# Layer three of a graph network: edge tables in two fp16 terms with a lift per feature, ten gathered tiles a block instead of eleven

## The reference

```python
h_edge = concatenate([h[src], h[dst]], axis=-1)
m_ij = relu(h_edge @ W_interact + b_interact)            # one row per edge
m_i = segment_sum(m_ij, src, num_segments=6250) / sqrt(16)
x = x + (h + relu((h + m_i) @ W_update + b_update))      # h + ... is the layer's own residual
```

## Time and profile before

| | |
|---|---|
| time, median of 3 runs | 1647.03 us (1644.14 to 1647.19) |
| the profiled execution: time, span | 1644.32 us, 1642.5 us |
| TensorE, matmuls | 1429.2 us busy, 87% |
| VectorE | 1394.0 us, 85% |
| ScalarE | 1009.9 us, 61% |
| GpSimd | 999.7 us, 61% |
| granted TensorE clock, mean | 0.952 of full speed |

### The profile page before, as it was taken

One profiled execution on the slowest core, in us unless ns is written; L12 is line 12 of the kernel. 1 busy time (PEld: TensorE's weight loads), 2 busy tenths in 40 slices (PEclk: granted clock), 3 DMA queues, 4 the chain that ended last, 5 costly groups with the idle time before them and its releaser, 6 DMA issues. The chain is left out here.

```text
span 1642.5 us, 43233 instructions
## 1 busy us (share of the span) xinstructions
PE 1429.2 (87%) x16208; PEld 1228.5 (75%) x16208; DVE 1394.0 (85%) x4293; ACT 1009.9 (61%) x1990; POOL 999.7 (61%) x1033
## 2 busy tenths in 40 slices
PE   1614888999999989999996499999999999999997
PEld 1302666777777667777776499999999999999997
DVE  7968797999999347777767599999999999999997
ACT  1724676787778520000005388888888878788885
POOL 4363606787850027777702677777777777777773
PEclk9855899999999999999997799999999999999999
DMA  3004725564653169999961244444454444444442
GB/s 114 1 1 120 277 105 195 196 240 173 223 209 134 29 203 300 301 309 306 292 204 35 71 114 115 122 113 123 114 123 121 115 116 112 113 121 115 122 115 61
DMA packets 125002, 245.15 MB, mean 149 GB/s; under 512 B 21784, under 2 KB 76201, under 8 KB 124794
## 3 DMA queue, kind: packets, MB, share of 16 engines
q1 hardware_dynamic: 95179, 184.46, 33.6%
q0 software_dynamic: 28032, 57.34, 14.0%
q10 hardware_dynamic: 1584, 0.59, 0.1%
HBM read 172.37 MB, written 73.14 MB: 149 GB/s over the span
## 5 line engine op out<-in xcount | busy, mean ns | idle before, releaser
L1427 PE MATMUL ps<-slab,room 125*128 125x128 bf16 x6762 | 435.6, 219 | 0.0
L987 ACT ACTIVATE slab<-ps 128x980 f16<-128x980 f32 x256 | 321.3, 1277 | 118.3 <-PE ps L1200 103.1
L1427 PEld LDWEIGHTS ps<-slab,room 125*128 125x128 bf16 x6762 | 393.1, 98 | 0.0
L899 POOL DMA_INDIRECT cells<-b_rows,work x319 | 305.8, 959 | 97.0 <-issue 91.4
L1099 ACT ACTIVATE lnw<-iota_w,keys 128x126 f32<-128x126 f32 x900 | 290.9, 389 | 1.6 <-POOL slab L890 1.6
L1418 PE MATMUL ps<-inv,hot 125*128 125x128 bf16 x2700 | 260.5, 221 | 3.7 <-DVE hot L2097 3.7
L1211 PE MATMUL ps<-slab,room 128*128 128x320 f16 x1568 | 252.2, 301 | 0.1
L1227 PE MATMUL ps<-slab,room 128*128 128x320 f16 x1568 | 225.0, 299 | 0.0
L1200 PE MATMUL ps<-hot 128*128 128x245 bf16 x1024 | 161.7, 283 | 49.3 <-DVE hot L1765 38.5
L859 POOL DMA_INDIRECT hot<-t_rows,pairs x160 | 165.7, 1036 | 51.7 <-issue 48.2
L1227 PEld LDWEIGHTS ps<-slab,room 128*128 128x128 f16 x1568 | 152.6, 98 | 58.3 <-issue 2.7
(11 more groups left out here) (346 smaller groups left out, 2284.4 us busy)
## 6 DMA issues: line engine op xcount, KB each, us to landing
slabs_d<-slab SPq DMA_DIRECT2D x14, 3920.0 KB, 13.2
slab<-slabs_d SPq DMA_DIRECT2D x98, 560.0 KB, 5.2
hot<-lane_d SPq DMA_DIRECT2D x50, 576.0 KB
keys<-up_d SPq DMA_DIRECT2D x50, 128.0 KB
inv<-inv_row SPq DMA_DIRECT2D x32, 160.0 KB
cells<-b_rows,work POOLq DMA_INDIRECT x319
keys<-down_d SPq DMA_DIRECT2D x50, 96.0 KB
t_rows<-room SPq DMA_DIRECT2D x1, 3200.0 KB, 13.7
```

Source lines behind the costliest of these rows:

```text
L899: p.indirect_dma_start(rows_g[gi % RS][:, j, :], None, b_rows, bass.IndirectOffsetOnAxis(ap=node_t[:, t:t + 1], axis=0)).then_inc(e_gath[g ...
L987: a.activation(slab[par][:, :, u * UB * BW:(u + 1) * UB * BW].rearrange("p h (k d) -> p k h d", k=UB), psum_unit(u).rearrange("p k (h d) - ...
L1427: last = t.matmul(to, end_hot[g // 3][0:BN, u:u + P], bt[0:BN, bt_at(tile, w), k, :], start=False, stop=w == w1 - 1 and k == TERMS - 1)
```

## The change

The tables of layer three come in two fp16 terms instead of three bf16 ones (`a_terms`, `bt`: the high term and what is left). So that fp16's range suffices, each feature is multiplied by a power of two: `lift_of_edges` on VectorE makes the powers from the norms of the columns of `W_interact` and the bias and multiplies the weights and the bias by them, and `keep_sum` divides by them again, and by the 4 of sqrt(16). The one-hots of lanes and ends are fp16.

Tile 4 is picked too: 8 tiles are picked, 10 fetched. The messages of groups 0, 2 and 5 (`SPLIT_GROUPS`) are two fp16 terms with an fp16 one-hot; those of groups 1, 3 and 4 are plain f32 with an f32 one-hot, without a low term. VectorE instead of ScalarE makes the one-hots of the source of groups 2 and 5 (`DVE_HOTS`). The lanes' one-hots are made in one piece of 2304 columns. The high term of a block's `a` is made by ScalarE, the low one by VectorE. In the preparation, ScalarE's middle term and one of GpSimd's two subtractions go.

```diff
-    GROUPS = (((0,), (4, 5)), ((1,), (6, 7)), ((2, 3), (8,)), ((15,), (9, 10)), ((16,), (11, 12)), ((17,), (13, 14)))
-    UP, DOWN = (0, 1, 2, 3), (15, 16, 17)
+    GROUPS = (((0, 1), (5,)), ((2, 3), (6,)), ((4,), (7, 8)), ((15,), (9, 10)), ((16,), (11, 12)), ((17,), (13, 14)))
+    UP, DOWN = (0, 1, 2, 3, 4), (15, 16, 17)
+    SPLIT_GROUPS = (0, 2, 5)
+    DVE_HOTS = (2, 5)
...
@@ ScalarE, second_layer
+                    if (s, u) == (1, 2):
+                        a.activation(edge_sq, w_ab[:, :], ACT.Square).then_inc(u_lift, 1)
+                    if (s, u) == (1, 9):
+                        act.wait_ge(s_once, ONCE_REACH)
+                        a.activation(edge_sq, ps[:, 2, 0:2 * D], ACT.Sqrt, scale=EDGE_REACH).then_inc(u_lift, 1)
@@ TensorE, second_layer
+                        if (s, u) == (1, 5):
+                            pe.wait_ge(u_lift, 4)
+                            t.matmul(ps[:, 2, 0:2 * D], ones[:, :], edge_sq, start=True, stop=True).then_inc(s_once, 1)
+                        if (s, u) == (2, 0):
+                            pe.wait_ge(u_lift, 5)
@@ VectorE, second_layer
+                        if (s, u) == (1, 13):
+                            lift_of_edges()
@@ VectorE
+            def lift_of_edges():
+                dve.wait_ge(u_lift, 5)
+                link(v.scalar_tensor_tensor(out=drop_f, in0=b_i, scalar=-1.0, in1=b_i, op0=ALU.mult, op1=ALU.max))
+                link(v.tensor_tensor(out=lift_f, in0=edge_sq[:, 0:D], in1=edge_sq[:, D:2 * D], op=ALU.add))
+                link(v.tensor_tensor(out=lift_f, in0=lift_f, in1=drop_f, op=ALU.add))
+                link(v.tensor_scalar(lift_f, lift_f, 1e-30, 1e30, ALU.max, ALU.min))
+                link(v.tensor_scalar(drop_b, lift_b, 23, None, ALU.arith_shift_right))
+                link(v.tensor_scalar(lift_b, drop_b, -1.0, float(2 * 127 + TOP), ALU.mult, ALU.add))
+                link(v.tensor_scalar(drop_b, drop_b, -float(TOP + 2), None, ALU.add))
+                link(v.tensor_scalar(lift_b, lift_b, 23, None, ALU.logical_shift_left))
+                link(v.tensor_scalar(drop_b, drop_b, 23, None, ALU.logical_shift_left))
+                for k in range(2):
+                    v.tensor_tensor(out=w_ab[:, k * D:(k + 1) * D], in0=w_ab[:, k * D:(k + 1) * D], in1=lift_f, op=ALU.mult)
+                v.tensor_tensor(out=b_i, in0=b_i, in1=lift_f, op=ALU.mult)
+                link(v.tensor_tensor(out=edge_sq[:, 0:D], in0=drop_f, in1=ident[:, :], op=ALU.mult))
+                link(v.tensor_reduce(out=settle[:, :], in_=edge_sq[:, 0:D], op=ALU.add, axis=AX.X))
+                nc.vector.sem_inc(u_lift, 1)
...
-                    for k in range(GB):
-                        piece = row_lane[0:BN, b % 2, k * GW:(k + 1) * GW]
-                        last = v.tensor_scalar(piece, piece, up_c[0:BN, 0:1], None, ALU.is_equal)
-                    last.then_inc(e_rowhot, 1)
+                    lanes_of = row_lane[0:BN, b % 2, :]
+                    v.tensor_scalar(lanes_of, lanes_of, up_c[0:BN, 0:1], None, ALU.is_equal).then_inc(e_rowhot, 1)
...
+            def source_hot(gi):
+                if gi % GB not in DVE_HOTS:
+                    return
+                if gi > 5:
+                    dve.wait_ge(e_psum, gi - 5)
+                b, at = gi // GB, DVE_HOTS.index(gi % GB)
+                both = [P, GT, BE // 2, 2]
+                v.tensor_tensor(out=src_hot[gi % 6].rearrange("p j (w e) -> p j w e", e=2),
+                                in0=iota_hi[:, 0:BE].rearrange("p (w e) -> p w e", e=2).unsqueeze(1).to_broadcast(both),
+                                in1=lane_twice[:, b, at, :, :].unsqueeze(2).to_broadcast(both), op=ALU.is_equal
+                                ).then_inc(e_dvehot, 1)
...
             for gi in range(NGR):
                 b, g = divmod(gi, GB)
                 add_rows(gi)
                 if gi + AHEAD < NGR:
                     prepare(gi + AHEAD)
                 low_term(gi)
-                if g < 2 and b + 1 < NB:
-                    split_a(b + 1, 2 * g)
-                    split_a(b + 1, 2 * g + 1)
+                if gi + AHEAD < NGR:
+                    source_hot(gi + AHEAD)
+                if g == 2 and b + 1 < NB:
+                    split_lo(b + 1)
@@ TensorE, edge_sum and source_sum
-                    for k in range(TERMS):
+                    for k in range(HALVES):
                         last = t.matmul(to, lanes_of, a_terms[0:BN, b % 2, k, :],
...
                 for j in range(GT):
-                    last = t.matmul(ps[0:BE, 4 + b % 2, 0:2 * D], src_hot[gi % 6][:, j, :],
-                                    msg[gi % 3][:, j, :, :].rearrange("p k f -> p (k f)"),
+                    of = msg_split[gi % 3][:, j, :, :].rearrange("p k f -> p (k f)") if split else msg[gi % 3][:, j, :]
+                    last = t.matmul(ps[0:BE, 4 + b % 2, 0:2 * D if split else D], src_hot[gi % 6][:, j, :], of,
@@ GpSimd, preparation
-                    p.tensor_tensor(out=brest[0:BN, bk % 2, :, :], in0=bslot[0:BN, c % 2, :, :], in1=to[:, :, 0, :],
-                                    op=ALU.subtract).then_inc(f_brest, 1)
-                if bk is not None:
-                    pool.wait_ge(f_bmid, bk + 1)
-                    p.tensor_tensor(out=to[:, :, 2, :], in0=brest[0:BN, bk % 2, :, :], in1=to[:, :, 1, :],
+                    p.tensor_tensor(out=to[:, :, 1, :], in0=bslot[0:BN, c % 2, :, :], in1=to[:, :, 0, :],
                                     op=ALU.subtract).then_inc(f_blo, 1)
```

More of the change, by code:

```diff
@@ L63, in gnn_kernel @@
     REACH = 260.0
-    assert LIFT * LIFT * D < 65504.0 ** 2 and REACH > 2 * D
+    EDGE_REACH = 130.0
+    assert LIFT * LIFT * D < 65504.0 ** 2 and REACH > 2 * D and EDGE_REACH > D
     MAGIC = 12582912.0
@@ L356, in gnn_kernel @@
-        a_rest = scaled[:, D:2 * D]
-        assert TERMS * D <= 2 * SC and 2 * D <= SC
+        bt_all = slab[1][:, :, :].rearrange("p h n -> p (h n)")
+        bt = bt_all[:, 0:BTN * HALVES * D].rearrange("p (t k f) -> p t k f", k=HALVES, f=D)
+        o, o1 = 2 * NB * D, BTN * HALVES * D + 2 * GW
+        end_hot = [room_b.bitcast(f16)[:, o:o + HOT_UNITS[0] * P], bt_all[:, o1:o1 + HOT_UNITS[1] * P]]
+        assert o + HOT_UNITS[0] * P <= NT * TERMS * P and o1 + HOT_UNITS[1] * P <= HI * SC
+        assert NT * D + GW <= HI * SC // 2 and KU * FH + 8 + GW <= 3 * KW // 2
@@ new lines, in gnn_kernel @@
+        msg_f = [slab_f[0][:, NT * D:NT * D + GW], work[:, KU * FH + 8:KU * FH + 8 + GW],
+                 slab_f[1][:, BTN * HALVES * D // 2:BTN * HALVES * D // 2 + GW]]
+        msg = [x.rearrange("p (j f) -> p j f", j=GT) for x in msg_f]
+        msg_split = [x.bitcast(f16).rearrange("p (j k f) -> p j k f", j=GT, k=2) for x in msg_f]
+        row_lane = hot_b.bitcast(f16)[:, 0:2 * CAP].rearrange("p (s n) -> p s n", s=2)
+        a_kept = table_f[:, 0:NB * D].rearrange("p (t f) -> p t f", f=D)
@@ L521, in chunk, with splits, hots @@
             return hT[:, c * CW:(c + 1) * CW]
+        def splits(gi):
+            return sum(g % GB in SPLIT_GROUPS for g in range(gi + 1))
+        def hots(gi):
+            return sum((g % GB in DVE_HOTS) == (gi % GB in DVE_HOTS) for g in range(gi + 1))
         STAGE, TURN, FLIP = "stage", "turn", "flip"
@@ L1101, in source_hot, with split_hi @@
                 last.then_inc(e_far, 1)
-                act.wait_ge(e_far, gi + 1)
-                a.activation(src_hot[gi % 6], far, ACT.Relu, scale=-0.25, bias=quarter[:, 0:1]).then_inc(e_srchot, 1)
+                act.wait_ge(e_far, hots(gi))
+                a.activation(src_hot[gi % 6], far, ACT.Relu, scale=-1.0, bias=unit_c[:, 0:1]).then_inc(e_srchot, 1)
+            def split_hi(b):
+                if b > 1:
+                    act.wait_ge(e_sum, (b - 1) * GB)
+                a.activation(a_terms[0:BN, b % 2, 0, :], a_kept[0:BN, b, :], ACT.Copy).then_inc(f_aterm, 1)
             act.wait_ge(q_lane, 1)
             act.wait_ge(f_blo, len(ends_at))
+            act.wait_ge(f_aok, NC)
+            split_hi(0)
             for gi in range(SOON):
@@ L1416, in edge_sum @@
                     lanes_of = row_lane[0:BN, b % 2, tile * P:(tile + 1) * P]
-                    for k in range(TERMS):
+                    for k in range(HALVES):
                         last = t.matmul(to, lanes_of, a_terms[0:BN, b % 2, k, :],
-                                        start=k == 0, stop=not picked and k == TERMS - 1)
+                                        start=k == 0, stop=not picked and k == HALVES - 1)
                     if picked:
@@ L1425, in edge_sum @@
                             u = unit[w, tile] * P
-                            for k in range(TERMS):
+                            for k in range(HALVES):
                                 last = t.matmul(to, end_hot[g // 3][0:BN, u:u + P], bt[0:BN, bt_at(tile, w), k, :],
-                                                start=False, stop=w == w1 - 1 and k == TERMS - 1)
```

(15 more changed lines are left out.)

117 lines of the change are left out of this document (57 added, 60 removed).

## The result

The changed kernel takes 1623.5 us (median of 4 runs, 1621.9 to 1626.57) against 1646.38 beside it: a ratio of 0.9867, 95% interval 0.9852 to 0.9882. It is faster, by 1.3%. The forecast was 1574 with a range from 1560 to 1603: the sign was right, the size was not. Its profiled execution took 1626.57 us with a span of 1624.8, so 17.7 us less span than before, not 71.2.

The account below looks back on a forecast made before the run. The prediction took GpSimd and TensorE as both full before, GpSimd alone after. Terms of -63.1, -10.3, -2.2, +4.4 and 0 us sum to -71.2: span 1571.3, time 1573.1, against the median 1575.8, stated as 1574, range 1560 to 1603.

Parts of the forecast that it names:

- What bound the kernel before: Edge stage: GpSimd, issuing without a break at 13.88 us a block, and TensorE, needing 13.6, were both full.
- Costs: Edge stage after the change, work a block: TensorE 11.8 us (12.0 with gaps), VectorE 11.4.
- The step that failed: Edge stage: ten gathers at 12.62 us a block make GpSimd alone the pace; fifty gathers fewer save 63.1 us.
- the second term: End of the edge stage: 13.5 us from last gather to end instead of 23.8, so -10.3 us.
- Rival (b): Edge stage: TensorE, VectorE or their order still sets 12.8 to 13.2 us a block, 1589 at 13.0; chance 0.22.
- 1.262 us for a gather: Edge stage: the time from one gather's issue to the next, taken over unchanged from the earlier trace.
- rival (c): Edge stage: long VectorE operations hold up gathers; 1643 if all is lost, 1608 if half; chance 0.08.
- the rule set against the change: Edge stage: some VectorE instructions take the shared SBUF port pair, so long compare and source one-hots could stop gathers' descriptors.
- The lift: Layer two, slab 1: linked VectorE operations scaling the edge tables delay the exact path, +4.4 us, between 0 and +6.
- The start of gathers: Preparation: gathers begin earlier as a subtraction and a middle term go, then b's store limits; -2.2 us, between 0 and -4.
- The start of the kernel: Kernel start: ten small iotas more on GpSimd and a longer plan row, ahead of a long wait: 0 us.
- rival (d): Edge stage: TensorE's clock drops in idle gaps, making it slower, 1710 if in a quarter of blocks; chance 0.04.

Follow-up runs that it names:

- before_six: The kernel before the change, but each group fetches one tile of rows, 6 gathers a block instead of 11, part of the sum left out: 1635.31 us.
- three_six: Changed kernel with new orders for ScalarE's work ahead, VectorE's low term and the adding to `hT`, and only 6 gathers a block, other rows left out: 1526.18 us.
- act_order: Changed kernel with ScalarE making the high term of the next `a` one group earlier and source one-hots four groups ahead instead of two: 1585.03 us.
- dve_order: Changed kernel with VectorE making the source one-hot and the next block's low term of `a` before the present group's low term: 1590.55 us.
- no_lift: Changed kernel without the lift of the edge tables: no powers of two, no product, Square and Sqrt for them: 1619.94 us.
- three_halves: Changed kernel with new orders for ScalarE, VectorE's low term and the adding to `hT`, lanes' compare in two separate pieces of 1152 columns: 1584.27 us.
- act_dve: Changed kernel with the new orders of both act_order and dve_order, without the early adding to `hT`: 1586.81 us.
- three_pieces: Changed kernel with new orders for ScalarE, VectorE's low term and the adding to `hT`, lanes' compare in six back-to-back pieces of 384 columns: 1589.84 us.
- act_halves: act_order with the lanes' compare in two pieces of 1152 columns, at groups 0 and 3, instead of one of 2304: 1580.23 us.

## Why the prediction was right or wrong

**What bound the kernel before: right.** GpSimd issued without a break and TensorE was just below it; before_six gained 9 us. (Between the first gather and the last lie 550 issues, not 549; the 551 intervals and the 1.262 us are right.)

**Costs: right.** TensorE 11.8 us a block for 11.8, VectorE 11.6 for 11.4 (three_six).

**The step that failed:** "This is more than 12.0 and 11.4. So after the change GpSimd alone sets the pace, and TensorE's saving below 12.6 is worth nothing." The second sentence doesn't follow from the first. It takes the largest of three sums, as if each engine could always work ahead. In the changed kernel VectorE waits, in each block, for the message of group 2, which stands on ScalarE behind a one-hot of the source and the high term of `a` (which the change moved there), and that wait stands ahead of everything of the next group 0. This costs 13.49 - 12.9 = 0.6 us a block against GpSimd's real pace, and since VectorE is behind at the end, it keeps the 10.3 us of the second term too. act_order shows it: without a saving of work, it takes 38 us off and brings that term back. dve_order, which changes only VectorE's side of the loop, takes 33 off. The mistake behind it is the line on ScalarE, "it has the most room and is left out": its share of 64% says nothing of when the message comes. Rival (b) named the kind of thing ("the order between them"), and priced it from 12.8 to 13.3; but it took 5 us off at the end, where the changed kernel ended 25.3 us after its last gather and not within 13.5.

**A term that was too small: 1.262 us for a gather.** With GpSimd as the bound it is 1.278 to 1.306. Of rival (c) that much is real, and with it the rule set against the change: 50 x 10 x (1.289 - 1.262) = 13.5 us in act_order. The forecast with it, 1576 + 13.5 = 1589, lies among what the kernels with ScalarE's or VectorE's order repaired gave, 1580 to 1593. I had excluded it by a mean over short bf16 compares, none of 0.81 us.

**Other terms.** The lift: +4.4 forecast, +4.1 measured, and no_lift gives 3.7 of it back at the very place. The start of gathers: -5.1 for -2.2, of the right kind, the wait named there being the store (2.13 us for `b_rows`). The start of the kernel: +2.9 is no part of the change, for the first slab product of layer two begins anywhere from 595.9 to 599.7 us in the seventeen traces of this case, whose kernels differ only later, with before and before_six at 596.8 and 597.7. The clock: 0.98 with TensorE at 90%, so rival (d) stayed out. The mean issue in the changed kernel was 0.99 us, just under the 1.0 that the prediction gave as the sign of (c).

## What to carry to other kernels

When an edit takes work off the engine that bounds, don't only compare sums: walk one round of the in-order lists, and for each wait ask what its partner has in front of the thing waited for, and what stands behind the wait. If no engine is full after the edit, look for a loop, and first move the wait behind ready work: three such moves of a few lines each were worth 15, 33 and 38 us here, each alone, where the whole change had brought 23. If gathers are the bound, try to spread a long VectorE operation, with other work between the pieces (8.3 us in three_halves).

## What the runs showed of the hardware that was not expected

A gather's issue, mostly 0.94 us, lasts up to 1.98 us (act_dve) when it meets a VectorE compare of 0.81 us. In act_order those that started ahead of the compare and were held up end 0.12 us after it, and those that started 0.08 to 0.40 us behind its start end 0.81 to 0.82 us after its end. Behind the first of six compares of 384 columns back to back it lasts 1.46 us (three_pieces). Where it met a compare of 1152 columns it took 1.29 at most in act_halves. Two kernels with the same work and GpSimd as the bound differ by 7.6 us, in part by where these meet. A gather's rows can also land later than the 2.56 us of the earlier trace rows: the chain of act_order has one landing of 4.48 us, and no run here tells why.

```profile
1211.81 0.30 issue
1212.12 4.48 DMA cell_hi<-b_rows,work
```
